# Second attention with relative positions: packed relative values, products grouped by how the array is split, band moved in 64-row pieces, output stored by tile

## The reference, cut to what matters

```python
dist  = jnp.clip(idx[None, :] - idx[:, None], -R, R) + R      # R = 64
pe_k  = rel_emb_k[dist]                                       # [256, 256, 8]
pe_v  = rel_emb_v[dist]
q     = q / jnp.sqrt(hd)                                      # hd = 8
score = einsum('bhqd,bhkd->bhqk', q, k) + einsum('bhqd,qkd->bhqk', q, pe_k)
attn  = softmax(score, axis=-1)
ctx   = einsum('bhqk,bhkd->bhqd', attn, v) + einsum('bhqk,qkd->bhqd', attn, pe_v)
out   = ctx @ W_out + b_out
```

## Time and profile before

| what | value |
|---|---|
| median of 3 runs | 1679.4 us (1679.25 to 1684.8) |
| profiled execution, span | 1677.5 us |
| mean granted TensorE clock | 0.976 |
| TensorE busy | 1552.2 us, 93% |
| VectorE busy | 904.4 us, 54% |
| ScalarE busy | 732.4 us, 44% |
| second attention, first relative scores to last instruction | 1102.3 to 1668.9 us |

### The profile page before, as it was taken

How to read it: one execution, slowest core, us unless ns; L and a number is a source line. 1 busy time by engine, 2 the same in 40 slices (tenths; PEclk the granted TensorE clock), 3 DMA queues, 4 the chain that set the end, 5 groups by cost and what they waited for, 6 DMA issues and landing times. The chain is left out here.

```text
span 1677.5 us, 38807 instructions
## 1 busy us (share of the span) xinstructions
PE 1552.2 (93%) x14424; PEld 1233.4 (74%) x14424; DVE 904.4 (54%) x3193; ACT 732.4 (44%) x1975; POOL 299.0 (18%) x376
## 2 busy tenths in 40 slices
PE   6899999999999999999599999959999999999996
PEld 5668888888888888888365656537777777777764
DVE  5336545454545454545322222237877777777774
ACT  2322222222222222222223232258888888888873
POOL 2010201111111101010430000003323332333232
PEclk9999999999999999999699999979999999999998
DMA  4009400000000000000243232258889998899886
GB/s 118 0 8 86 105 8 7 8 8 6 6 6 5 7 5 7 3 10 4 85 114 114 77 112 85 72 166 245 250 241 251 237 250 235 246 246 254 236 235 173
DMA packets 234032, 181.50 MB, mean 108 GB/s; under 512 B 82703, under 2 KB 223913, under 8 KB 233888
## 3 DMA queue, kind: packets, MB, share of 16 engines
q1 hardware_dynamic: 228514, 167.17, 37.1%
q0 software_dynamic: 5376, 12.44, 2.7%
HBM read 103.63 MB, written 75.78 MB: 107 GB/s over the span
## 5 line engine op out<-in xcount | busy, mean ns | idle before, releaser
L1547 ACT ACTIVATE a1Pm<-a1Pm,a1nmx 128x256 f32<-128x256 f32 x512 | 255.5, 504 | 0.4 <-DVE a1nmx L1609 0.3
L1609 DVE CUSTOM_DVE_ANT_0 a1Pm<-a1ps_S,a1Sb 128x256 f32<-128x256 f32 x512 | 196.1, 421 | 77.2 <-issue 75.5
L768 DVE TENSOR_TENSOR a0AT<-a0ps_AM,mask 128x384 f32<-128x384 f32 x256 | 125.5, 551 | 192.5 <-PE a0ps_AM L588 192.1
L773 DVE TENSOR_TENSOR a0MT<-a0ps_AM,mask 128x384 f32<-128x384 f32 x256 | 138.4, 555 | 88.2 <-PE a0ps_AM L609 85.1
L1542 ACT ACTIVATE a1Rt<-a1ps_R 128x384 f32<-128x384 f32 x264 | 128.6, 487 | 106.7 <-PE a1ps_R L1407 96.9
L1162 DVE TENSOR_TENSOR f1hid<-f1ge,f1ps_b 128x512 f32<-128x512 f32 x80 | 55.0, 688 | 192.1 <-PE f1ps_b L1095 182.4
L1426 PE MATMUL a1ps_T<-ident,a1Pm 128*128 128x128 f32 x1024 | 155.9, 275 | 0.0
L607 PE MATMUL a0ps_AM<-a0AT 128*128 128x256 f32 x512 | 152.9, 380 | 0.0
L572 PE MATMUL a0ps_qk<-xnT_all,a0w_in 128*128 (+1 forms) x512 | 138.3, 393 | 2.0 <-PEq L151 1.3
L715 ACT ACTIVATE a0qk<-a0ps_qk 128x512 f32<-128x512 f32 x128 | 76.4, 597 | 119.3 <-PE a0ps_qk L572 119.3
L1407 PE MATMUL a1ps_R<-rel_st,a1stk 72*128 72x192 bf16 x528 | 90.0, 253 | 35.5 <-ACT a1Rt L1542 13.2
(11 more groups left out here) (246 smaller groups left out, 2991.0 us busy)
## 6 DMA issues: line engine op xcount, KB each, us to landing
skew<-a1Rt SPq DMA_DIRECT2D x132, 384.0 KB, 5.4
a1Sb<-skew SPq DMA_DIRECT2D x131, 384.0 KB, 7.0
a1stk<-parts SPq DMA_DIRECT2D x153, 64.0 KB
a1stk<-parts SPq DMA_DIRECT2D x51, 192.0 KB
parts<-a1prt SPq DMA_DIRECT2D x18, 384.0 KB
f1w<-in_L_ffn_w_kernel SPq DMA_DIRECT2D x16, 344.0 KB
f1w<-in_L_ffn_w_kernel SPq DMA_DIRECT2D x16, 320.0 KB
f1wo<-in_L_ffn_wo_kernel SPq DMA_DIRECT2D x16, 320.0 KB
```

Of the source, the lines that this page charges most:

```text
L768: nc.vector.tensor_tensor(AT[i][h][:, :], ps_AM[i][h][:, 0:HB], mask[:, :], ALU.mult).then_inc(A_ready, 1)
L773: nc.vector.tensor_tensor(MT[i][h][:, :], ps_AM[i][h][:, 0:HB], mask[:, :], ALU.mult).then_inc(M_ready, 1)
L1547: nc.scalar.activation(Pm[:, place(h), :], Pm[:, place(h), :], ACT.Exp, bias=nmx[it][:, h:h + 1], scale=-1.0, accum_out=den[it][:, h:h + 1 ...
L1609: nc.vector.tensor_tensor_reduce(out=Pm[:, place(h), :], in0=ps_S[hp % 2][:, n, :], in1=bias_of(it, hp, n), scale=-1.0, scalar=3.0e38, op0 ...
```

## The change

Five things change, all in the second attention.

1. `rel_values`: a group with one table no longer gets a table of zeros for the other half. Its two head halves `w` go to the two halves of the rows instead. The rows that are not written hold old numbers; both banks are zeroed once at the start, and `pick` has a second form that takes, for each quarter, only the half that was written.
2. The order on TensorE: `rel_values` 0 and 1 stand together in pair 3, 2 and 3 in pair 5, and all of `weigh` in pair 4.
3. The band: each send and fetch becomes two DMAs of 64 rows. One of the two halves carries 192 columns, the other 128. The pitch in DRAM goes from 319 to 320.
4. `Sb` becomes two buffers, one for even and one for odd tiles, each of 256 columns; the zero parts outside the band differ for each half of the rows. VectorE clears those of the first, GpSimd those of the second. TensorE waits for VectorE's clearing before its first relative scores.
5. `store_stage` goes. SyncE stores tile `s-3` in `step` after fetch 3, and the last three tiles at the end.

```diff
-                nc.gpsimd.tensor_tensor(pick[:, :], wide[:, 0:GH1], wide[:, GH1:GI], ALU.add).then_inc(pool_made, 1)
-                nc.gpsimd.memset(tabs[:, len(TABLES), :], 0.0).then_inc(pool_made, 1)
+                for n in range(2):
+                    for w in range(2):
+                        nc.gpsimd.tensor_copy(pick[:, 1, 2 * n + w, :], wide[:, (1 - w) * GH1:(2 - w) * GH1]).then_inc(pool_made, 1)
+                for n in range(4):
+                    nc.gpsimd.tensor_tensor(pick[:, 0, n, :], wide[:, 0:GH1], wide[:, GH1:GI], ALU.add).then_inc(pool_made, 1)
...
-PITCH = BAND + P - 1
+PITCH = BAND + P
...
-        Sb = m.sb("a1Sb", [P, HP, 2 * REL + BAND, 2])
+        Sb = [m.sb(f"a1Sb{i}", [P, HP, T, 2]) for i in range(2)]
...
+        def band_of(it, half):
+            keys = slice(0, P + half * REL) if it == 0 else slice(REL + half * REL, T)
+            return slice(half * REL, (half + 1) * REL), keys
+        def outside(it, half):
+            rows, keys = band_of(it, half)
+            return Sb[it][rows, :, keys.stop:T, :] if it == 0 else Sb[it][rows, :, 0:keys.start, :]
+        def tables_of(it, ig):
+            return [(t, jt) for t, (i2, jt, g2) in enumerate(TABLES) if (i2, g2) == (it, ig)]
...
-                        use = [(t, jt) for t, (i2, jt, g2) in enumerate(TABLES) if (i2, g2) == (it, ig)]
-                        if len(use) == 1:
-                            use.append((len(TABLES), use[0][1]))
+                        use = tables_of(it, ig)
                         for w in range(2):
                             at = ig * GI + w * GH1
+                            c = (1 - w) * (P // 2)
                             for half, (t, jt) in enumerate(use):
-                                c = (1 - w) * (P // 2)
+                                half = w if len(use) == 1 else half
                                 rows = slice(half * (P // 2), (half + 1) * (P // 2))
...
-                            if 2 <= hp < 6:
+                            if hp in (3, 5):
+                                rel_values(s - 1, prev_b, pit, hp - 3)
                                 rel_values(s - 1, prev_b, pit, hp - 2)
-                            if 3 <= hp < 7:
-                                weigh(s - 1, prev_b, pit, hp - 3)
+                            if hp == 4:
+                                for q in range(QUAD):
+                                    weigh(s - 1, prev_b, pit, q)
...
+                pe.wait_ge(sm["cleared"], 1)
                 pe.wait_ge(sm["loaded"], 16 * 3)
...
+                    kind = len(tables_of(it, 2 * k)) % 2
-                    nc.vector.tensor_tensor(out, ps_X[k % 2], bc(bc(pick[:, :], 1, H1), 1, 4), ALU.mult).then_inc(sm["X_ready"], 1)
+                    nc.vector.tensor_tensor(out, ps_X[k % 2], bc(pick[:, kind, :, :], 2, H1), ALU.mult).then_inc(sm["X_ready"], 1)
...
                 nc.vector.memset(vx[:, :, :, :, :], 0.0)
-                nc.vector.memset(Sb[:, :, 0:REL, :], 0.0)
-                nc.vector.memset(Sb[:, :, REL + BAND:2 * REL + BAND, :], 0.0).then_inc(sm["cleared"], 1)
+                nc.vector.memset(ps_X0[:, :, :, :], 0.0)
+                nc.vector.memset(ps_p[:, :, :], 0.0)
+                for half in range(2):
+                    ins = nc.vector.memset(outside(0, half), 0.0)
+                ins.then_inc(sm["cleared"], 1)
                 v.wait_ge(sm["cleared"], 1)
+                v.wait_ge(sm["edge_cleared"], 2)
...
-                pool.wait_ge(sm["cleared"], 1)
+                for half in range(2):
+                    nc.gpsimd.memset(outside(1, half), 0.0).then_inc(sm["edge_cleared"], 1)
+                    pool.wait_ge(sm["edge_cleared"], half + 1)
...
+                def store(s):
+                    sp.wait_ge(sm["combined"], s + 1)
+                    sp.dma_start(out_tiles[:, s, :], x_all[:, s, :]).then_inc(sm["stored"], 16)
...
-                    c0 = 0 if it == 0 else 2 * (P - 1)
-                    sp.dma_start(skew[it][:, ps, c0:c0 + 2 * BAND], Rt[:, ps, :, :].rearrange("p n c h -> p n (c h)")).then_inc(skew_out[q], 16)
+                    for half in range(2):
+                        rows = slice(half * REL, (half + 1) * REL)
+                        cols = slice((1 - half) * REL, BAND) if it == 0 else slice(0, BAND - half * REL)
+                        c0 = 2 * cols.start + (0 if it == 0 else 2 * P)
+                        wide = 2 * (cols.stop - cols.start)
+                        sp.dma_start(skew[it][rows, ps, c0:c0 + wide],
+                                     Rt[rows, ps, cols, :].rearrange("p n c h -> p n (c h)")).then_inc(skew_out[q], 16)
...
-                    sp.dma_start(Sb[:, ps, REL:REL + BAND, :].rearrange("p n c h -> p n (c h)"),
-                                 bass.AP(flat.tensor, flat.offset + 2 * (q * PQ * PITCH + P - 1),
-                                         [[2 * (HP * PITCH - 1), P], [2 * PITCH, PQ], [1, 2 * BAND]])).then_inc(skew_in[q], 16)
+                    for half in range(2):
+                        rows, keys = band_of(it, half)
+                        at = (P - 1 if it == 0 else P - REL) + keys.start - rows.start
+                        sp.dma_start(Sb[it][rows, ps, keys, :].rearrange("p n c h -> p n (c h)"),
+                                     bass.AP(flat.tensor, flat.offset + 2 * ((rows.start * HP + q * PQ) * PITCH + at),
+                                             [[2 * (HP * PITCH - 1), REL], [2 * PITCH, PQ], [1, 2 * (keys.stop - keys.start)]])).then_inc(skew_in[q], 16)
...
                     fetch_band(s, it, 3)
+                    if s >= 3:
+                        store(s - 3)
                     fill(1)
...
-                sp.wait_ge(sm["cleared"], 1)
...
-def store_stage(nc, x_all, out):
...
-                sp.dma_start(out.rearrange("b (t p) d -> p (b t) d", p=P), x_all[:, :, :]).then_inc(stored, 16)
-                sp.wait_ge(stored, 16)
+                for n in range(last - 2, last + 1):
+                    store(n)
+                sp.wait_ge(sm["stored"], 2 * B * 16)
```

More of the change, by code:

```diff
@@ L562, in _ @@
                         scatter_group(b // 2 - 1, 0)
-                pool.wait_ge(pool_made, 7)
+                pool.wait_ge(pool_made, 13)
             @block.tensor
@@ L978 @@
 ZW = 16
-ZP = SLOTS // P * ZW // (2 * (P - 1))
+ZP = SLOTS // P * ZW // (2 * P)
 CLEARS = D // ZW + 2 * 8 // ZP
@@ L987, in clear_dram @@
                      zeros[:, :, :]).then_inc(zeroed, 16)
-    some = zeros[:, :, :].rearrange("p a b -> p (a b)")[:, 0:ZP * 2 * (P - 1)].rearrange("p (n c) -> p n c", n=ZP)
+    some = zeros[:, :, :].rearrange("p a b -> p (a b)")[:, 0:ZP * 2 * P].rearrange("p (n c) -> p n c", n=ZP)
     for p in range(0, HP, ZP):
         sp.dma_start(skew[0][:, p:p + ZP, 2 * BAND:2 * PITCH], some).then_inc(zeroed, 16)
-        sp.dma_start(skew[1][:, p:p + ZP, 0:2 * (P - 1)], some).then_inc(zeroed, 16)
+        sp.dma_start(skew[1][:, p:p + ZP, 0:2 * P], some).then_inc(zeroed, 16)
 def ffn1_stage(nc, w0_d, w1_d, wo_d, slots_dram, eo_dram, xn_all, send_ids, sent, ident, x_all, b_out, xnT_all, front, parts, one, bias_q, bias_k):
@@ L1213, in __init__ @@
                  "stacked_k0 stacked_k1 S_done S_ready P_ready T_done Ta_ready Tv_ready X_done X_ready c_done cT_ready rrep_ready "
-                 "rdT_done rdT_ready y_done y_added pool_step vec_step cleared ids_ready rows_in first_added combined").split()
+                 "stored rdT_done rdT_ready y_done y_added pool_step vec_step cleared edge_cleared ids_ready rows_in first_added combined").split()
         names += [f"skew_out{q}" for q in range(QUARTERS)]
@@ L1323, in attn1_stage @@
     skew, parts = a["skew"], a["parts"]
+    out_tiles = a["out"].rearrange("b (t p) d -> p (b t) d", p=P)
     S2 = 2 * B
@@ L1539, in keep_R @@
                     if hp % PQ == 0:
-                        act.wait_ge(skew_in[hp // PQ], s * 16)
+                        act.wait_ge(skew_in[hp // PQ], s * 32)
                     nc.scalar.activation(Rt[:, hp, :, :], ps_R[:, :, :].rearrange("p n c -> p c n"), ACT.Copy).then_inc(sm["R_ready"], 1)
@@ L1602, in add_scores @@
                     if hp % PQ == 0:
-                        v.wait_ge(skew_in[hp // PQ], (s + 1) * 16)
+                        v.wait_ge(skew_in[hp // PQ], (s + 1) * 32)
                     v.wait_ge(sm["S_done"], s * HP + hp + 1)
@@ L1608, in add_scores, with pick_diagonal @@
                         h = 2 * hp + n
-                        nc.vector.tensor_tensor_reduce(out=Pm[:, place(h), :], in0=ps_S[hp % 2][:, n, :], in1=bias_of(it, hp, n),
+                        nc.vector.tensor_tensor_reduce(out=Pm[:, place(h), :], in0=ps_S[hp % 2][:, n, :], in1=Sb[it][:, hp, :, n],
                                                        scale=-1.0, scalar=3.0e38, op0=ALU.add, op1=ALU.min,
                                                        accum_out=nmx[it][:, h:h + 1]).then_inc(sm["S_ready"], 1)
-                def pick_diagonal(s, k):
```

(25 more changed lines are left out.)

5 lines of the change are left out of this document (1 added, 4 removed).

## The result

The changed kernel takes 1700.6 us (median of 4 runs, 1700.3 to 1703.4) against 1679.7 us before: a ratio of 1.0123, with a 95% interval of 1.0099 to 1.0147. The forecast was 1655, in a range of 1640 to 1684. What happened is rival (a), "SyncE's issues take the bound", to which the prediction gave 1702 us and a chance of 0.14.

A forecast was written before the change was run, and what follows sets the result against it. TensorE and SyncE's loop for the query fills were taken as two equal bounds. 1677.5 - 21.7 (loop) + 6.5 (start) - 9.0 (end) - 0.3 (last tile's folding) = 1653.0, plus 1.9 to the median: 1655 us, range 1640 to 1684.

The forecast's parts named there:

- rival (a): Second attention's loop: seven more SyncE issues at 0.45 us make two tiles 35.0 us, time 1702 us; chance 0.14.
- TensorE: Second attention: packing and grouping save 1.8 us a tile; two tiles then take 31.5 us by TensorE.
- (d): Rival: ScalarE does not hold TensorE, so 56 us are gained in the tiles, time 1620 us; chance 0.04.
- (e): Rival: packed halves do not run side by side, only grouping gains; two tiles 32.8 us, time 1668 us; chance 0.01.
- The price of a half's issue: SyncE's band DMAs: issuing one half costs 0.3 to 0.45 us, taken as 0.4.
- Where it decides: SyncE's loop: rival (a) decides from about 0.5 us an issue with landings not below 4.2 us.
- Issue or data: From first query fill to scores: 12.0 us by data, 14.6 by issue; 12.5 taken.
- backlog: DMA queues: the 13.25 us from first fill to scores looks like queued data and shrinks to about 12.0.
- Issues ahead of `parts`: SyncE's loop: from the odd tile's first relative scores to the issue of `parts` stays 13.2 us.
- Start: Start of second attention: TensorE's first scores wait for VectorE's clearing; +6.5 us with second halves (5 to 7.5).
- End: End of the kernel: 64 KB instead of 2 MB left to store; -9.0 us (-5.5 to -11.5).
- The stores: SyncE's loop: one store among five more issues from first to ninth fill, each half's issue taken at 0.4 us.

The follow-up runs named there:

- e3_pall: Changed kernel with whole 128-row band transfers, TensorE's wait for clearing moved later, loop parts, fills and stores issued by GpSimd: 0.9732 of kernel before, about 1635 us.
- e1_heads: Changed kernel with as many band transfers, cut by head pair (128 rows, 192 columns) instead of 64-row halves: 0.9997 of kernel before, about 1679 us.
- e1_wide: Changed kernel with its 64-row halves each carrying all 192 columns: 1.0228 of kernel before, about 1718 us.
- e2_whole_late: Changed kernel with whole 128-row band transfers and one store at the end instead of loop stores: 0.9876 of kernel before, about 1659 us.
- e1_late: Changed kernel without stores in the loop, all tiles stored in one transfer at the end: 1.0085 of kernel before, about 1694 us.
- e2_halves: Kernel before with only the 64-row halves, pitch of 320, two band tiles and their clearing added: 1.0129 of kernel before, about 1701 us.
- e1_whole: Changed kernel with each band send and fetch again one transfer of 128 rows and 192 columns: 0.9895 of kernel before, about 1662 us.
- e2_pool: Changed kernel with whole 128-row band transfers and the loop's parts and fills issued by GpSimd: 0.9839 of kernel before, about 1653 us.

## Why the prediction was wrong, step by step

- **TensorE: right.** Even tiles were forecast in pairs of 0.8, 1.4, 2.0, 3.2, 2.8, 2.0, 0.8, 2.7 and ran in 0.83, 1.38, 1.78, 3.24, 2.81, 1.95, 0.83, 2.73. The odd tile's 0.8, 2.9, 1.0, 2.2, 3.0, 2.8, 0.8, 2.2 shows as soon as nothing stops it: 0.82, 3.00, 0.95, 2.17, 2.87, 2.83, 0.83, 2.18 in e3_pall. The 31.5 us for two tiles were 31.2 in the best pairs there, 31.7 in the median. Rivals (d) and (e) fall.
- **The price of a half's issue: the step that failed.** "A half may cost from 0.3 (fewer rows) to 0.45, and I take 0.4, near the row": it costs 0.59 to 0.62, outside both bounds. I had taken the band's own row for the nearest. But the same group held a row that speaks for shape: three fills of 8 rows and 64 KB take 2.09 us, 0.70 each, more than a band of 128 rows and 384 KB at 0.45. So fewer rows and fewer bytes did not make an issue cheaper already in the kernel before, and the upper bound should have been 0.70.
- **Where it decides: half right.** The prediction put the turning point of rival (a) at "about 0.5 us an issue with landings not below 4.2". e1_heads lies below it at 0.45 and is as fast as the kernel before, though 1.0% slower than with whole transfers; e1_wide lies above it at 0.61, and its fills' loop is 2.7 us longer than that of e1_heads. But the last landing fell to 2.1, so the condition on landings was wrong. With 0.60 in the prediction's own sum the run comes to 9.0 + 4 x 0.75 + 0.6 = 12.6 (12.7 measured), and rival (a) would have been the forecast.
- **Rival (a) was right in kind, and its 1702 us is partly luck.** It had 0.45 us an issue (0.59 to 0.62 measured) and a last landing of 4.2 (2.1 measured), too little and too much, and counted seven more issues; the loop of 35.0 then came near the 35.5 measured.
- **Issue or data: the choice followed.** From the first fill to the scores I set bounds of 12.0 (data) and 14.6 (issue) and took 12.5; it measured 12.7 + 2.1 = 14.8. What I called a backlog rested on the 5.9 and 7.0 of the earlier trace rows, which are medians of one quarter each; over all quarters a landing took 5.1 and 5.0, and with halves a quarter was complete 4.1 and 4.4 after its first issue. Against the mean loop before (9.1 + 4.7) the run took 3.6 more, and the last landing gave only 2.6 back.
- **Issues ahead of `parts`: miscounted.** "Its issue stays at 13.2", with two second halves on the way; it came at 16.5, against a mean of 14.1 before. Between the odd tile's first scores and `parts` SyncE has six pairs of halves and a store to issue, not two more issues, and it comes to them late from the tile before. The landing of `parts` fell more than forecast, to 4.3 instead of 6.5.
- **The stop's own cost** was not in the sum of any case: TensorE's clock falls to 1.2 GHz (granted 0.50) in the stop, and tile 9 is longer by the 3.36 us of the stop and 1.4 us more.
- **Start: right.** First scores 6.6 us later, counted from the stage before (13.66 against 7.06); +6.5 was forecast. On the axis it is 4.1, because the stage before ended 2.5 us sooner; over the runs here that end moves between 1090.3 and 1095.2.
- **End: right.** The last sum ends at 1698.7 and the span 3.0 us later; 2.9 was forecast. The end is 8.4 us shorter in all.
- **Sum.** With every term as measured (-2.5 is the earlier end of the stage before, which was not forecast) the sum is 1677.5 + 27.9 + 6.6 - 2.5 - 8.4 = 1701.1, beside a span of 1701.7. The term that was wrong is the loop's: -21.7 forecast, +27.9 measured.
- **The stores** had been priced as one issue of 0.4 in the run; by the estimates above each took 0.4 to 0.8 us of the loop with whole transfers (e2_whole_late) and 0.4 with halves (11 us for 29, e1_late).

The Trainium skill (DMA: Bandwidth & Descriptors, "Rules for kernel authors") was cited against this change: two transfers to partition halves are not worth it. The trace agrees with the advice (1.0129 for the halves alone, e2_halves). Its reason, the shared engines, is not the larger part here: e1_heads and e1_wide share them alike, with the same bytes, and differ by 2.3% with issues of 0.45 and 0.61 us. The same page of the Trainium skill ("Issuing engines are not separate DMA queues") says that issuing from several engines saves only the time on the sequencer, usually small beside the transfer. It is not small here: SyncE issued for 15.4 us without a break, and e3_pall, which moves fills and stores to GpSimd, is faster than e1_whole.

## What to carry to other kernels

Before a transfer is cut in pieces, price an issue by its shape from every row that the trace has on that queue, not from the transfer that is cut. If the issuing engine runs without a break for longer than a landing takes, bytes saved buy little: here they were worth about 1%, and the second issues cost more. List all that an in-order queue must issue between two events of a loop, and ask who waits for the second piece. When a median to landing is read, ask how many of the transfers it counts. Then the part of a change that works is best kept, and issues are moved to an engine with time: whole transfers turned a loss of 1.2% into a gain of 1.0%, and GpSimd's issues with the early start made it 2.7%.

## What the hardware showed that I had not expected

- SyncE's time for one issue goes by shape and hardly by bytes. As medians it is 0.32 us (192 KB) and 0.36 (384 KB) for 128 rows after a pause, 0.44 to 0.51 when it follows another issue at once, 0.59 to 0.61 for 64 rows in both cases (128 KB and 192 KB alike), 0.66 to 0.70 for a fill of 8 rows. It is not by rows alone: a key fill of 24 rows mostly takes 0.43. Why is open.
- The store of 128 rows of 512 bytes takes 0.59 us on SyncE in the changed kernel and 0.43 in e1_heads, where no 64-row transfer stands ahead of it. But in e1_whole and e2_pool, which have none either, the median is 0.71 and 0.56. What sets it is open.
- GpSimd issued nine query fills in 5.4 us (e2_pool), 0.60 each, less than SyncE's 0.7; its key fills of 24 rows took 0.75, more than SyncE's 0.43.
